# Sending all rows of the last routed group ahead of the first addition on GpSimd

## The reference, cut to what matters

```python
rh = jax.nn.relu(features @ router_w1 + router_b1)
expert_logits = jax.nn.softmax(rh @ router_w2 + router_b2, axis=-1)
top_w, top_i = jax.lax.top_k(expert_logits, TOP_K)
routing_weights = jax.nn.softmax(top_w, axis=-1)
...
combined = jnp.sum(sel * routing_weights[..., None], axis=2)
...
x = x + combined
```

## Time and profile before

| | |
|---|---|
| timed runs | 2229.14, 2219.26, 2229.53 us; median 2229.14 |
| profiled execution | 2220.27 us, span 2218.5 us |
| mean granted TensorE clock | 0.923 |
| busy share of the span | PE 84%, DVE 76%, ACT 65%, POOL 54% |
| row writes on GpSimd (L1951) | 100, 100.4 us busy |
| additions on GpSimd (L1971) | 108, 171.2 us busy, 134.3 us idle ahead of them |
| scaling on VectorE (L2171) | 108, 47.5 us busy, 142.8 us idle ahead of them |
| median time from issue to landing | 3.5 us for a row write, 3.9 us for an addition |

### The profile page before, as it was taken

One profiled execution on the slowest core, in us unless ns is written; L12 is line 12 of the kernel. 1 busy time (PEld: TensorE's weight loads), 2 busy tenths in 40 slices (PEclk: granted clock), 3 DMA queues, 4 the chain that ended last, 5 costly groups with the idle time before them and its releaser, 6 DMA issues. The chain is left out here.

```text
span 2218.5 us, 49553 instructions
## 1 busy us (share of the span) xinstructions
PE 1856.9 (84%) x10024; PEld 1491.2 (67%) x10024; DVE 1689.0 (76%) x5423; ACT 1441.6 (65%) x4425; POOL 1201.3 (54%) x1164
## 2 busy tenths in 40 slices
PE   3888857599954999999999999999999556999995
PEld 2444435377743778877878778878877455778884
DVE  7898879877754788888888889888898655455553
ACT  5567558244412889889889889889889663333331
POOL 2010000056565777777777777777774167755553
PEclk9999979599856999999999999999999768999997
DMA  4322101021103444444443444444442454655551
GB/s 144 95 76 60 53 24 52 19 83 49 42 23 84 121 119 119 122 119 117 122 118 111 120 114 117 123 117 117 122 117 69 148 172 136 118 117 89 101 92 26
DMA packets 133895, 215.45 MB, mean 97 GB/s; under 512 B 42813, under 2 KB 89084, under 8 KB 133604
## 3 DMA queue, kind: packets, MB, share of 16 engines
q0 software_dynamic: 61920, 132.16, 24.9%
q1 hardware_dynamic: 67022, 72.68, 10.7%
q10 hardware_dynamic: 4662, 7.46, 1.1%
HBM read 150.28 MB, written 56.51 MB: 93 GB/s over the span
## 5 line engine op out<-in xcount | busy, mean ns | idle before, releaser
L1394 POOL DMA_INDIRECT area<-wh_table,area x788 | 769.9, 977 | 260.2 <-issue 235.0
L1721 PE MATMUL bank<-area 128*126 x1960 | 484.2, 390 | 31.0 <-ACT area L1641 15.3
L1721 PEld LDWEIGHTS bank<-area 128*126 128x126 f32 x1960 | 349.8, 188 | 103.8 <-issue 55.1
L1427 DVE TENSOR_SCALAR area<-iota_row,area 128x126 f32<-128x126 f32 x980 | 355.0, 369 | 24.5 <-ACT area L1594 17.3
L1627 ACT ACTIVATE area<-iota_row,area 128x126 f32<-128x126 f32 x735 | 285.8, 389 | 0.0
L1971 POOL DMA_INDIRECT out_dram<-area x108 | 171.2, 1585 | 134.3 <-DVE area L2171 115.7
L1641 ACT ACTIVATE area<-area 128x126 f32<-128x126 f32 x735 | 237.0, 386 | 0.4
L590 POOL DMA_INDIRECT sorted_slots<-area x112 | 134.9, 1204 | 115.9 <-DVE area L946 85.4
L1580 ACT ACTIVATE area<-bank 125x512 bf16<-125x512 f32 x245 | 145.4, 593 | 79.2 <-DVE area L1441 76.1
L1741 PE MATMUL bank<-area 128*128 128x250 f32 x800 | 189.1, 380 | 6.8 <-ACT area L1648 3.7
L1502 DVE SCALAR_TENSOR_TENSOR acc_mem<-acc_mem,area,bank 125x258 f32 x245 | 117.8, 481 | 97.0 <-PE bank L1709 82.4
(11 more groups left out here) (417 smaller groups left out, 4050.4 us busy)
## 6 DMA issues: line engine op xcount, KB each, us to landing
area<-moe_rows SPq DMA_DIRECT2D x54, 264.0 KB, 2.9
area<-wh_table,area POOLq DMA_INDIRECT x788
area<-area SPq DMA_DIRECT2D x17, 388.5 KB
wh_table<-area SPq DMA_DIRECT2D x50, 126.5 KB
xn<-in_x_dram SPq DMA_DIRECT2D x25, 250.0 KB
xt_rows<-area SPq DMA_DIRECT2D x50, 125.0 KB, 2.5
area<-xt_rows SPq DMA_DIRECT2D x25, 250.0 KB
x_rows<-area SPq DMA_DIRECT2D x25, 250.0 KB
```

Of the source, the lines that this page charges most:

```text
L1394: g.indirect_dma_start(out=gath[:, (i + GT) % RS, :], out_offset=None, in_=table, in_offset=bass.IndirectOffsetOnAxis(ap=idx_tab[:, i:i + ...
L1427: ins = V.tensor_scalar(xm[:, b, t, :], iota_row[:, :], rowl[:, j % 10, t:t + 1], fetched(j, D)[:, t:t + 1], ALU.is_equal, ALU.mult)
L1721: last = T.matmul(bank[US[b]][0:RW, 0:WROW], sm[:, b, t, :], gath[:, bass.ds(place + t, 1), 0:WROW].rearrange("p a w -> p (a w)"), start=( ...
```

## The change

One number changes:

```diff
-AHEAD_OF_ADDS = 3
+AHEAD_OF_ADDS = 12
```

## The result

The changed kernel takes 2240.7 us (median of 12 runs, 2230.6 to 2247.2) against 2223.18 us (12 runs, 2216.6 to 2229.53): 1.008 times the time before, 95% interval 1.006 to 1.0101. That is 17.5 us more (the interval stands for 13 to 22), where 17.0 were forecast.

What follows compares the result with a forecast made beforehand. VectorE waiting for GpSimd's late additions at expert boundaries, TensorE pacing between them, was taken as the bound; 23.04 − 0.45 − 5.56 = 17.03 us on the 2229.14 median gave 2246 us, range 2235 to 2253.

Steps and rivals of the forecast that it cites:

- The price of the piece: Ahead of tile 0's addition: eighteen writes at 1.28 us each delay tiles 1 and 2 by 23.04 us.
- The second step: Between tiles 2 and 3: TensorE gains slack but loses 2.80 us to its clock, leaving a gain of 0.45 us.
- the row of tiles 13 to 15: Trace of an expert boundary without writes, 11.60 us against 17.16 from tile 7 to 9; basis for the 5.56 us gain.
- The backlog: At tile 8: GpSimd's lateness from writes between additions goes, gaining 5.56 us between tiles 7 and 9.
- The sum: Over the expert stage: 23.04 less 0.45 less 5.56, so 17.03 us slower.
- The level: Whole kernel: the shift was added to the median of three timed runs, 2229.14 us, giving 2246; lower runs would give 2237.
- Shorter landings: Rival: three additions land faster without writes in the same queue, 3.7 us come back, 2242 us; chance 0.06.
- The full price: Rival: TensorE stays at 1.2 GHz or loses GpSimd's gain at a boundary; 22 to 24 us slower, 2252; chance 0.12.
- The three buffers: Rival: only tile 3 waits, for tile 0's landing; 4.9 us slower, 2234, within 0.5%; chance 0.06.
- A cheap piece: Rival: the eighteen writes issue at under 0.33 us each, time 2229; chance 0.02, shared with an edit that does nothing.

Runs made afterwards that it cites:

- no_first_boundary: The changed kernel with the additions of tiles 0 and 1 sent onto unread scratch tables, so no tile waits for them on account of its expert; one run 2225.94 us.
- price_twice: The kernel before, with its nine in-loop blocks also sent ahead of the additions into a second table that nobody reads; one run 2249.36 us.
- tensor_kept_busy_75: The changed kernel with 75 products that nobody reads added in TensorE's list just ahead of tile 2's third product; one run 2237.05 us.

## Why the prediction was right, point by point

**The price of the piece was right.** 23.04 us were worked out; 23.09 and 23.14 stand at tiles 1 and 2. It went on in full because of the two boundaries, shown by no_first_boundary.

**The second step was mis-sized.** The gain at tile 3 was 0.59 for 0.45, but that is luck. The clock loss was 1.58 us instead of 2.80 (TensorE's timeline of the changed kernel):

```profile
1897.55 0.60 PE L2349 MATMUL bank<-ident,area 128*128 128x128 f32 x4
1917.79 3.48 PE L2384 MATMUL bank<-area 128*128 128x256 f32 x8 [19.64 <-DVE area L2145]
1921.11 1.89 PE L2360 MATMUL bank<-area 128*128 128x256 f32 x8
```

After 19.64 us of standing still one group of eight ran at half clock and the next at full, a shorter loss than the row I took (14.94 us gap) and nearly that of the row which I passed over (3.46 for 1.90 behind a gap of 4.16 us). A loss that small would, in the prediction's own working, have put tile 3 at 3.47 us behind tile 2. It came at 4.44, by VectorE's own turn. So two things failed in this step: the clock loss, which was taken too large, and the bound, which counted TensorE from the weight copy on and left VectorE's list between two scalings out. VectorE's turn held up tile 3 only. TensorE had started tile 3's product 1.26 us behind tile 2's scaling, as the bound had it, and tile 4 follows tile 3 by 4.81 us and not by 5.64: 0.83 us more came back there. Together it is 1.42, near the step's upper end of 1.56, and not 0.45.

**The backlog.** 5.56 us were expected between tiles 7 and 9, and 4.95 came (21.73 to 16.78); another 0.93 came at tile 10, which the row of tiles 13 to 15 had not shown me. Together 5.88. From tile 7 to 10 it takes 16.91 us, three of TensorE's turns of 5.64: once GpSimd keeps up, the boundary costs nothing there. price_twice ties this to the writes in the loop.

**The sum.** 17.03 were worked out and 15.88 are there at tile 14; the difference is in the main tiles 4 and 10. The longer landings behind tile 14, which the prediction did not have, made 18.21 of it in this profile, and the timed medians are 17.5 apart. That they agree with 17.0 to half a microsecond is partly luck: too small a gain and landings left out go opposite ways, and the interval of 13 to 22 us tells none of these sums apart. That the distance from tile 9 to the end would stay at 278 us was nearly so: 280.5.

**The level.** I took the two groups of timed runs, 2219 and 2229 us, for two levels and put the forecast onto the upper one, 2246. With 12 runs the kernel before spreads evenly from 2216.6 to 2229.5, so 2240.7 is the same shift from a median that is 6.0 lower. Tile 0's scaling alone moves by 12.4 us between profiles.

**The rivals.** Shorter landings did not come: tile 0's took 3.89 us in the chain of the changed kernel with no write behind it, where it had taken 3.84. Its last write stood just ahead of it; the additions of tiles 1 and 7, 8 and 42 us behind the last write, took 4.1 to 4.2 us from issue to landing, where 4.12 and 3.87 stood before. And of the three landings that the prediction counted into the path, only tile 0's still sets the pace in the changed kernel. Its chain at tile 0's addition:

```profile
1910.57 1.61 POOL out_dram L1971
1912.48 3.89 DMA out_dram<-area
```

The fit of the Trainium skill, "DMA: Bandwidth & Descriptors", section "Anatomy of one DMA — SWDGE (gpsimd) path", gives 2.3 us for it as an estimate; the trace has 3.89, and 4.1 to 4.2 with no write near, so the difference is not time spent behind the writes. The full price failed, as 7.2 us came back. The three buffers alone would have made the 4 us that no_first_boundary shows. A cheap piece is out: the last write of the piece still takes 0.97 us and 0.30 of issue.

## What to carry to other kernels

Work that is moved out of a loop to its front costs its full length if the front is on the chain, and wins only what it had held up in the loop; price both before moving. Look which waits inside the loop already cover such work (here one or two writes behind each tile), and fill these instead of choosing between all ahead and two behind each. For a bound on how fast one engine can follow a release, count the whole list of every engine in the cycle, not only of the one that was late, and look one tile further whether the delay lasts.

## What the runs showed of the hardware

TensorE's clock has two levels here, 1.2 and 2.4 GHz. In tensor_kept_busy_75 it fell in a gap of 3.55 us, behind 16.91 us of unbroken work, and the loss (2.87 us) was larger than after a gap of 19.64 us in the changed kernel (1.58) or of 4.16 us in the kernel before (1.56). In these three places the length of the gap did not set the loss.
